# Routed experts in a two-layer kernel: second half routed one step earlier, first group's weight rows spread by DMA out of SBUF instead of DRAM

## Chip, cores and metric

One NeuronCore of a Trainium2 chip. The metric is the device time of one execution in microseconds (us), the median of several. Engines: PE (TensorE), DVE (VectorE), ACT (ScalarE), POOL (GpSimd), and SP (SyncE), which here only issues DMAs. The core has 16 DMA engines.

## The reference

Input `x` has 1024 tokens of 256 numbers. Eight stages follow one another, each of them `x = x + stage(layernorm(x))`:

```
attention A, routed experts, attention B, routed experts,
attention C, small FFN, latent attention, small FFN
```

The change lies in the two "routed experts" stages (same weights both times):

```python
probs = softmax(x @ gate_w)                       # 1024 x 64
top_vals, top_idx = top_k(probs, 8)
rw = zeros(1024, 64); rw[token, top_idx] = top_vals / sum(top_vals)
g = einsum('th,ehi->tei', x, w_gate)              # 64 experts, 256 -> 96
u = einsum('th,ehi->tei', x, w_up)
h = silu(g) * u * rw[:, :, None]
out = einsum('tei,eih->th', h, w_down)            # 96 -> 256, summed over experts
```

All 64 experts are computed for all tokens. `rw` is zero where a token did not choose an expert.

## The kernel before, in words

Class `Moe` holds the expert stage, class `First` the order in which each engine runs it. The two stages are r = 0 and r = 1. The order of work on every engine is written out by hand; engines meet only through semaphores. Each method named below emits instructions on one engine.

**Tiling.** The 64 experts form 16 groups of 4. A group has 4 x 96 = 384 hidden channels, which are 3 blocks of 128 partitions (j = 0, 1, 2), and the tokens are cut in two halves of 512 columns (h = 0, 1). A *unit* is one block and one half, so a group has 6 units, in the order h = 0: j = 0, 1, 2, then h = 1: j = 0, 1, 2. Units 0, 1, 2 of the first group use the first half, units 3, 4, 5 the second.

**One unit.** `gate_up` (PE, L1308) makes 12 matmuls of 128x512, since a float32 product is made of three passes over high and low parts. `activate` (ACT, L1332) takes the silu. `weigh` (POOL, L1357) multiplies it with `e_rw`, the routing weights. `multiply` (DVE, L1377) multiplies with the up part and gives `e_inner`. `high_inner` (ACT, L1338) and `low_inner` (DVE, L1369) split that, and `down` (PE, L1323) makes 6 matmuls. On PE `down` of a unit follows `gate_up` of a unit two later; `gate_up` of unit u waits until `multiply` of unit u-2 is done, because the banks alternate. Beside this, ACT (`high_weights`, L1345) and POOL (`low_weights`, L1364) split one piece of the next group's weights in each unit.

**Routing weights as rows.** `weigh` needs, on each of the 128 partitions of a block, the row of 512 token weights of the expert to which the channel belongs. `e_rw` (128 x 3 x 1024) is that. It is filled by DMA:

- `logits` (PE), `route_begin` (DVE), `route_exp` (ACT), `route_end` (DVE: L1254 to L1264, eight top values, mask, normalization) give the weights of a half of the tokens with tokens on partitions.
- `turn_rows` (PE, L1271) transposes them, `copy_rows` (ACT, L1276) copies them to `rwT`, 64 partitions (one for each expert) x 1024.
- `store_rows` (SP, L1205) writes the half of `rwT` to DRAM, 64 rows of 2 KB, and waits until it has landed.
- `load_rows_of_half` (SP, L1211), for the first group only, reads each of the rows of experts 0 to 3 back, once for each destination partition. The six DMAs (`self.spans`) have 96, 32, 64, 64, 32 and 96 destination partitions: 384 rows of 2 KB, 786,432 bytes for a half.
- `load_rows` (SP, L1217) does the same from DRAM for every later group, with whole rows of 4 KB.

**Order around the change.** First half: its routing is done during the attention stage, `turn_rows` and `copy_rows` right behind it. SP then issues store and loads of half 0 and, in the same queue, the weights of group 1 (`load_group`, L1184 and L1189). Then it waits for half 1. PE runs units 0, 1 and 2 of the first group, between them the logits of the second half. The second half's routing runs on DVE among `multiply` and `low_inner` of units 0 and 1. `weigh` of unit 0 waits for the rows of half 0, `weigh` of unit 3 for those of half 1.

Of the kernel before, what the change touches and what calls it, by code (L numbers as in the profile page):

```python
# [20 lines left out]
HALF = 512  # L21
# [813 lines left out]
class Attend:  # L835
# [178 lines left out]
    def scalar(self, act, hook):  # L1014
# [21 lines left out]
        for what, *args in self.order:  # L1036
            if what == "rows":
                store_rows(*args)
            elif what == "scores":
                exponentiate(*args)  # L1040
            elif what == "store":
                store_sums(*args)
            elif what == "raw":
                self.raws.store(act, *args, self.ring_bank((what, *args)))
            elif what == "values":
                hook(*args)
# [63 lines left out]
class Moe:  # L1110
# [91 lines left out]
    def store_rows(self, sp, r, h):  # L1202
        cols = slice(h * HALF, (h + 1) * HALF)
        sp.wait_ge(self.rows_copied, 2 * r + h + 1)
        sp.dma_start(self.rw_dram[r][:, cols], self.rwT[:, cols]).then_inc(self.rows_stored, 16)  # L1205
        sp.wait_ge(self.rows_stored, 16 * (2 * r + h + 1))

    def load_rows_of_half(self, sp, r, h):
        cols = slice(h * HALF, (h + 1) * HALF)
        for j, e, a, b in self.spans:  # L1210
            sp.dma_start(self.rw[0][a:b, j, cols], self.rw_dram[r][e:e + 1, cols].broadcast_to([b - a, HALF])  # L1211
                         ).then_inc(self.r_first[h], 16)

    def load_rows(self, sp, r, i, s):
# [1022 lines left out]
class First:  # L2237
# [69 lines left out]
    def rows_and_groups(self, sp, r):  # L2307
        moe = self.moe
        first = moe.TURNS * r
        moe.store_rows(sp, r, 0)  # L2310
        moe.load_rows_of_half(sp, r, 0)
        moe.load_group(sp, r, first, 1)
        moe.store_rows(sp, r, 1)
        moe.load_rows_of_half(sp, r, 1)
        moe.load_rows(sp, r, first, 1)
        with sp.Fori(first + 1, first + moe.TURNS) as i:
            for s in range(2):
                moe.load_group(sp, r, i, s)
                sp.wait_ge(moe.weighted, moe.unit(i, moe.UNITS * (s - 1)))
                moe.load_rows(sp, r, i, s)  # L2320
        if r == 1:
            self.c.load(sp)
# [85 lines left out]
    def layer_of_tensor(self, pe, r, proj, ahead):  # L2408

        norm, out, moe, attend, early = self.norm, self.out, self.moe, self.attends[r], self.early[r]  # L2410
        E = self.EARLY
        use = 1 + 2 * r

        def hook(p, j):
            if (p, j) == early["turn"]:
                if r == 0:
                    pe.wait_ge(attend.max_done, attend.maxima)
                pe.wait_ge(attend.ctx_stored, 6)
                out.turn(pe, r, 0, E, attend.ctxs)
            if (p, j) == early["first"]:  # L2420
                if r == 0:
                    pe.wait_ge(proj.wo_loaded, 16)
                out.project(pe, r, 0, E, proj.wo)
            if (p, j) == early["second"]:
                out.project(pe, r, 2, E, proj.wo)
            if (p, j) == early["xT"]:
                norm.turn(pe, use, 0, E)
            if (p, j) == early["logits"]:
                norm.wait_stored(pe, use, 0)
                moe.logits(pe, r, 0, 1)  # L2430

        attend.tensor(pe, proj.wait_stacked, hook, ahead)
        first = moe.TURNS * r
        pe.wait_ge(attend.ctx_stored, 8)
        out.turn(pe, r, 1, (4, 5), attend.ctxs)
        pe.wait_ge(self.start.const_made, Start.CONSTS)
        moe.turn_rows(pe, r, 0, 3)
        out.project(pe, r, 4, (6, 7), proj.wo)
        out.project(pe, r, 6, (6, 7), proj.wo)
        moe.gate_up(pe, r, first, 0)  # L2440
        norm.turn(pe, use, 1, (6, 7))
        pe.wait_ge(moe.rows_copied, 2 * r + 1)
        moe.gate_up(pe, r, first, 1)
        norm.wait_stored(pe, use, 1)
        moe.logits(pe, r, 1, 6)
        moe.gate_up(pe, r, first, 2)
        moe.down(pe, first, 0, first=True)
        moe.down(pe, first, 1)
        moe.turn_rows(pe, r, 1, 7)
        moe.gate_up(pe, r, first, 3)  # L2450
        moe.down(pe, first, 2)
        moe.gate_up(pe, r, first, 4)
        pe.wait_ge(moe.rows_copied, 2 * r + 2)
        for u in range(5, moe.BODY):
            moe.gate_up(pe, r, first, u)
            moe.down(pe, first, u - moe.LAG, first=u == 5)
        with pe.Fori(first + 1, first + moe.TURNS - 1) as i:
            for u in range(moe.BODY):
                moe.gate_up(pe, r, i, u)
                moe.down(pe, i, u - moe.LAG)  # L2460
        last = first + moe.TURNS - 1
        for u in range(moe.BODY):
            moe.gate_up(pe, r, last, u)
            if u == moe.BODY - 1:
                moe.turn_sums(pe, r, 0)
            moe.down(pe, last, u - moe.LAG, final=u == 10)
        moe.down(pe, last, 10)
        moe.down(pe, last, 11, final=True)
        moe.turn_sums(pe, r, 1)
# [288 lines left out]
    def layer_of_vector(self, dve, r, ahead):  # L2758
        norm, out, moe, early = self.norm, self.out, self.moe, self.early[r]
        E = self.EARLY  # L2760
        use, first = 1 + 2 * r, moe.TURNS * r

        def sum_and_gather(t, banks):
            out.add(dve, r, t, banks)
            dve.wait_ge(out.added, 4 * r + t // 2 + 1)
            norm.gather(dve, use, t)
            norm.gather(dve, use, t + 1)

        def hook(p, j):
            if (p, j) == early["copy"]:  # L2770
                for k in range(KC):
                    out.copy_vector(dve, r, 0, k, E)
            if (p, j) == early["first"]:
                sum_and_gather(0, E)
            if (p, j) == early["second"]:
                sum_and_gather(2, E)
            if (p, j) == early["norm"]:
                norm.spread(dve, use, 0)
                norm.invert_by_newton(dve, use, 0)
                for t in range(4):  # L2780
                    norm.scale(dve, use, t)
            if (p, j) == early["xT"]:
                for k in range(KC):
                    norm.store_vector(dve, use, 0, k, E)
            if (p, j) == early["begin"]:
                moe.route_begin(dve, r, 0, 1)
            if r == 1 and (p, j) == (7, 4):
                moe.route_end(dve, r, 0)

        self.attends[r].vector(dve, hook, ahead)  # L2790
        if r == 0:
            moe.route_end(dve, r, 0)
        sum_and_gather(4, (6, 7))
        sum_and_gather(6, (6, 7))
        norm.spread(dve, use, 1)
        norm.invert(dve, use, 1)
        for t in range(4, 8):
            norm.scale(dve, use, t)
        norm.store_vector(dve, use, 1, 1, (6, 7))
        moe.multiply(dve, first, 0)  # L2800
        moe.low_inner(dve, first, 0)
        moe.route_begin(dve, r, 1, 6)
        moe.multiply(dve, first, 1)
        moe.low_inner(dve, first, 1)
        moe.route_end(dve, r, 1)
        moe.multiply(dve, first, 2)
        for u in range(3, moe.BODY):
            self.unit_of_vector(dve, first, u)
        with dve.Fori(first + 1, first + moe.TURNS - 1) as i:
            for u in range(moe.BODY):  # L2810
                self.unit_of_vector(dve, i, u)
        last = first + moe.TURNS - 1
        for u in range(moe.BODY - 1):
            self.unit_of_vector(dve, last, u)
        u = moe.BODY - 1
        moe.low_inner(dve, last, u - 1)
        moe.add(dve, r, 0)
        moe.multiply(dve, last, u)
        moe.add(dve, r, 2)
        moe.low_inner(dve, last, u)  # L2820
        dve.wait_ge(moe.added, 4 * r + 2)
        for t in range(4):
            norm.gather(dve, 2 + 2 * r, t)
# [420 lines left out]
```

## Time and profile before

| | |
|---|---|
| median of 3 runs | 1986.26 us (1985.53 to 1986.53) |
| the profiled execution | 1985.94 us |
| its span | 1984.2 us |
| PE busy | 1830.7 us, 92% |
| DVE, ACT, POOL busy | 1069.4, 919.3, 698.9 us |

A timeline row gives the start of an instruction (or of a run of equal ones) in us from the start of the span, its time in us, engine, line, operation and operands, and in brackets the idle time of the engine before it with what ended it. A row of stretches gives for each engine its busy time with the number of instructions, then the granted PE clock as a share of full speed, the mean busy share of the 16 DMA engines, and the GB/s that they moved. The two expert stages lie at about 208 to 621 us and 779 to 1192 us of the span, their entries at 204 to 240 and 774 to 810 us.

### The profile page before, as it was taken

To read this page: it belongs to the slowest core of one execution; us is meant where nothing else is said; L and a number is where in the kernel's file an instruction comes from. 1 tells how busy PE (TensorE), PEld (TensorE's weight loads), DVE (VectorE), ACT (ScalarE), POOL (GpSimd) and SP (SyncE) were. 2 spreads that over 40 slices of the span, in tenths; PEclk is the share of its full clock that TensorE was granted. 3 is DMA by queue.
4 is the path that set the end of the run, shared out by engine and by line. 5 is a ranking of instruction groups with operands and counts; after the bars stand their busy time and mean duration, and the time that the engine had idled before them with its cause. 6 is when DMAs were issued, how large, how long until landed. Compare 5 with 4: busy or idle time off the path is not lost. (4 is left out here: it accounts for less than half of the span.)

```text
span 1984.2 us, 30249 instructions
## 1 busy us (share of the span) xinstructions
PE 1830.7 (92%) x10564; PEld 1259.1 (63%) x10571; DVE 1069.4 (54%) x1785; ACT 919.3 (46%) x1947; POOL 698.9 (35%) x629
## 2 busy tenths in 40 slices
PE   6999899999998998999999996899979599999997
PEld 3333688888886555788888873333336377777785
DVE  6875444444445654444444456888754255555533
ACT  3676433333334665333333334487743245555521
POOL 5100366666663202566666643300010323232200
PEclk8999999999999999999999999899998599999997
DMA  4300444444430401544444422930010000000000
GB/s 125 89 1 1 126 111 109 110 107 110 108 91 23 114 2 43 136 109 108 108 109 110 110 58 66 135 77 1 1 22 0 0 1 2 1 1 1 1 1 22
DMA packets 136919, 121.71 MB, mean 61 GB/s; under 512 B 84305, under 2 KB 122665, under 8 KB 136585
## 3 DMA queue, kind: packets, MB, share of 16 engines
q1 hardware_dynamic: 136809, 120.24, 24.5%
q8 instruction: 69, 1.13, 0.2%
q14 instruction: 41, 0.34, 0.1%
HBM read 111.41 MB, written 8.65 MB: 61 GB/s over the span
## 5 line engine op out<-in xcount | busy, mean ns | idle before, releaser
L1369 DVE TENSOR_TENSOR e_inner_lo<-e_inner,e_inner_hi 128x512 fp32r<-128x512 f32 x192 | 247.4, 1289 | 390.7 <-ACT e_inner_hi L1338 390.5
L1357 POOL TENSOR_TENSOR e_wsilu<-e_silu,e_rw 128x512 f32<-128x512 f32 x192 | 261.5, 1362 | 225.8 <-ACT e_silu L1332 164.0
L1308 PE MATMUL psum<-e_x_hi,e_w_hi 128*128 128x512 f32 x768 | 304.1, 396 | 7.7 <-DVE e_inner L1377 7.7
L1308 PE MATMUL psum<-e_x_hi,e_w_lo 128*128 128x512 f32 x768 | 299.8, 390 | 0.0
L1308 PE MATMUL psum<-e_x_lo,e_w_hi 128*128 128x512 f32 x768 | 299.5, 390 | 0.0
L1332 ACT ACTIVATE e_silu<-psum 128x512 f32<-128x512 f32 x192 | 114.7, 597 | 346.5 <-PE psum L1308 346.5
L1364 POOL TENSOR_TENSOR e_w_lo<-e_raw,e_w_hi 128x384 fp32r<-128x384 f32 x180 | 221.1, 1228 | 129.1 <-ACT e_w_hi L1345 115.9
L1308 PEld LDWEIGHTS psum<-e_x_hi,e_w_hi 128*128 128x128 f32 x768 | 144.4, 188 | 49.1 <-DVE e_inner L1377 16.9
L1064 DVE TENSOR_REDUCE c_mx<-psum 128x1 f32<-128x1024 f32 x128 | 150.6, 1219 | 28.1 <-PE psum L933 27.6
L1308 PEld LDWEIGHTS psum<-e_x_hi,e_w_lo 128*128 128x128 f32 x768 | 144.6, 188 | 30.8
L1308 PEld LDWEIGHTS psum<-e_x_lo,e_w_hi 128*128 128x128 f32 x768 | 144.7, 188 | 29.1
L1323 PE MATMUL psum<-e_inner_hi,e_w_hi 128*128 128x512 f32 x384 | 150.5, 392 | 10.7 <-DVE e_inner_lo L1369 10.7
L1027 ACT ACTIVATE c_probs<-psum 128x512 f32<-128x512 f32 x256 | 136.4, 601 | 48.0 <-PE psum L965 45.6
L1377 DVE TENSOR_TENSOR e_inner<-psum,e_wsilu 128x512 f32<-128x512 f32 x192 | 130.6, 680 | 47.5 <-POOL e_wsilu L1357 47.5
L1323 PE MATMUL psum<-e_inner_hi,e_w_lo 128*128 128x512 f32 x384 | 149.5, 389 | 0.0
L1323 PE MATMUL psum<-e_inner_lo,e_w_hi 128*128 128x512 f32 x384 | 149.5, 389 | 0.0
L1345 ACT CAST e_w_hi<-e_raw 128x384 fp32r<-128x384 f32 x180 | 92.3, 513 | 122.4 <-PE psum L1323 122.0
L2150 DVE TENSOR_REDUCE l_negmax<-psum 128x1 f32<-128x256 f32 (+7 forms) x128 | 96.9, 757 | 91.3 <-PE psum L1990 90.7
L1338 ACT CAST e_inner_hi<-e_inner 128x512 fp32r<-128x512 f32 x192 | 117.7, 613 | 31.4 <-DVE e_inner L1377 31.4
L2127 POOL TENSOR_TENSOR l_q_whole<-l_rope,l_swap 64x512 f32<-64x512 f32 x32 | 40.8, 1275 | 220.3 <-DVE l_swap L2143 219.1
L2085 ACT COPY xn<-psum 128x512 f32<-128x512 f32 (+2 forms) x96 | 46.0, 480 | 126.6 <-PE psum L2002 126.6
L2077 ACT ACTIVATE l_probs<-psum,l_negmax 128x256 f32<-128x256 f32 (+7 forms) x128 | 95.3, 745 | 18.5 <-DVE l_negmax L2150 16.9
(366 smaller groups left out, 3262.4 us busy)
## 6 DMA issues: line engine op xcount, KB each, us to landing
e_rw<-e_rw_dram SPq DMA_DIRECT2D x60, 384.0 KB, 5.0
e_rw<-e_rw_dram SPq DMA_DIRECT2D x60, 256.0 KB, 5.3
e_raw<-in_L_ffn_w_gate SPq DMA_DIRECT2D x64, 192.0 KB, 2.6
e_raw<-in_L_ffn_w_up SPq DMA_DIRECT2D x64, 192.0 KB, 2.5
e_raw<-in_L_ffn_w_down SPq DMA_DIRECT2D x32, 384.0 KB, 3.5
e_rw<-e_rw_dram SPq DMA_DIRECT2D x68, 128.0 KB, 4.8
c_parts_dram<-c_part SPq DMA_DIRECT2D x8, 384.0 KB, 2.5
a_qs<-a_parts_dram SPq DMA_DIRECT2D x42, 64.0 KB, 2.3
```

Source lines behind the costliest of these rows:

```text
L1027: nc.scalar.activation(self.probs[:, self.step_of[p, j] % 2, x, 0:nq], self.ring_bank(("scores", p, j, x))[:, 0:nq], ACT.Exp, scale=HD ** ...
L1064: nc.vector.tensor_reduce(self.mx[:, p % 2, t % QUART, x:x + 1], self.max_buffer(n)[:, 0:cfg.max_width(t)], AX_X, ALU.max).then_inc(self.m ...
L1308: last = nc.tensor.matmul(bank[u % 2][:], self.w[a][s][:, KC * which + k, j * P:(j + 1) * P], self.x[b][:, k, h * HALF:(h + 1) * HALF], st ...
L1323: last = nc.tensor.matmul(self.obank[2 * h + m][:], flat[:, j * D + m * P:j * D + (m + 1) * P], self.inner_parts[b][:, u % 3, :], start=fi ...
L1332: self.core.nc.scalar.activation(self.silu[:, u % 2, :], self.gbank[u % 2][:], ACT.Silu).then_inc(self.silu_done, 1)
L1338: self.core.nc.scalar.copy(self.inner_parts[0][:, u % 3, :], self.inner[:, u % 2, :]).then_inc(self.high_made, 1)
L1357: self.core.nc.gpsimd.tensor_tensor(self.wsilu[:, u % 2, :], self.silu[:, u % 2, :], self.rw[s][:, j, h * HALF:(h + 1) * HALF], ALU.mult). ...
L1364: self.core.nc.gpsimd.tensor_tensor(self.w[1][1 - s][:, p, :], self.raw[:, p, :], self.w[0][1 - s][:, p, :], ALU.subtract).then_inc(self.w ...
L1369: self.core.nc.vector.tensor_tensor(self.inner_parts[1][:, u % 3, :], self.inner[:, u % 2, :], self.inner_parts[0][:, u % 3, :], ALU.subtr ...
L1377: self.core.nc.vector.tensor_tensor(self.inner[:, u % 2, :], self.ubank[u % 2][:], self.wsilu[:, u % 2, :], ALU.mult).then_inc(self.inner_ ...
L2077: nc.scalar.activation(probs[:, a, t % 2, 0:w], scores_of(a)[:, 0:w], ACT.Exp, bias=negmax[:, n % 4:n % 4 + 1], accum_out=sums[:, t // HT, ...
L2150: nc.vector.tensor_reduce(negmax[:, n % 4:n % 4 + 1], scores_of(a)[:, 0:(t + 1) * P], AX_X, ALU.max, negate=True).then_inc(negmax_ready, 1)
```

## The change

`load_rows_of_half` takes its source from `rwT` in SBUF and no longer from the copy in DRAM: one partition of 512 columns, repeated b - a times by a step of zero. So the loads need no longer wait for the store, and the wait is moved from `store_rows` to a place ahead of `load_rows`, which still reads DRAM. On PE, `turn_rows` of the second half is moved ahead of `down` of unit 1, and on DVE `route_end` of the second half is moved ahead of `low_inner` of unit 1. Number and size of the transfers stay the same.

```diff
         sp.dma_start(self.rw_dram[r][:, cols], self.rwT[:, cols]).then_inc(self.rows_stored, 16)
-        sp.wait_ge(self.rows_stored, 16 * (2 * r + h + 1))
 
     def load_rows_of_half(self, sp, r, h):
         cols = slice(h * HALF, (h + 1) * HALF)
         for j, e, a, b in self.spans:
-            sp.dma_start(self.rw[0][a:b, j, cols], self.rw_dram[r][e:e + 1, cols].broadcast_to([b - a, HALF])
+            sp.dma_start(self.rw[0][a:b, j, cols], self.rwT[e:e + 1, cols].unsqueeze(1).broadcast_to([1, b - a, HALF])
                          ).then_inc(self.r_first[h], 16)
@@ rows_and_groups
         moe.store_rows(sp, r, 1)
         moe.load_rows_of_half(sp, r, 1)
+        sp.wait_ge(moe.rows_stored, 32 * (r + 1))
         moe.load_rows(sp, r, first, 1)
@@ layer_of_tensor
         moe.gate_up(pe, r, first, 2)
         moe.down(pe, first, 0, first=True)
+        moe.turn_rows(pe, r, 1, 7)
         moe.down(pe, first, 1)
-        moe.turn_rows(pe, r, 1, 7)
         moe.gate_up(pe, r, first, 3)
@@ layer_of_vector
         moe.multiply(dve, first, 1)
+        moe.route_end(dve, r, 1)
         moe.low_inner(dve, first, 1)
-        moe.route_end(dve, r, 1)
         moe.multiply(dve, first, 2)
```

## Rows read from the trace of the kernel before

**Rows 1.** Stretches: PE in the steady part of the expert stage, and behind a gap.
```profile
260.00:285.00 25.00, 24.82 (x110) 20.19 (x109) 11.50 (x13) 9.22 (x18) 15.58 (x13) 1.00 0.43 111
803.00:807.00 4.00, 4.00 (x12) 3.10 (x12) 0.00 (x0) 0.00 (x0) 0.64 (x1) 0.57 0.88 247
```

**Rows 2.** Timeline of PE at both entries: start, time, line, operands [idle before <-releaser].
```profile
217.10 0.48 PE L1308 MATMUL psum<-e_x_hi,e_w_hi 128*128 128x512 f32 x1
223.31 0.50 PE L1323 MATMUL psum<-e_inner_hi,e_w_hi 128*128 128x512 f32 x1 [1.83 <-DVE e_inner_lo L1369]
225.67 0.63 PE L1271 MATMUL psum<-ident,xi 128*64 128x128 f32 x4 [0.71 <-DVE xi L1264]
226.05 0.47 PE L1308 MATMUL psum<-e_x_hi,e_w_hi 128*128 128x512 f32 x1
237.46 0.47 PE L1308 MATMUL psum<-e_x_hi,e_w_hi 128*128 128x512 f32 x1 [2.12 <-DVE e_inner L1377]
...
794.37 0.50 PE L1323 MATMUL psum<-e_inner_hi,e_w_hi 128*128 128x512 f32 x1 [2.42 <-DVE e_inner_lo L1369]
808.52 0.47 PE L1308 MATMUL psum<-e_x_hi,e_w_hi 128*128 128x512 f32 x1 [0.50 <-DVE e_inner L1377]
```

**Rows 3.** Timeline of POOL at both entries.
```profile
213.06 1.29 POOL L1357 TENSOR_TENSOR e_wsilu<-e_silu,e_rw 128x512 f32<-128x512 f32 x1 [14.88 <-DMA e_rw<-e_rw_dram]
235.32 1.26 POOL L1357 TENSOR_TENSOR e_wsilu<-e_silu,e_rw 128x512 f32<-128x512 f32 x1 [11.21 <-DMA e_rw<-e_rw_dram]
...
784.73 1.29 POOL L1357 TENSOR_TENSOR e_wsilu<-e_silu,e_rw 128x512 f32<-128x512 f32 x1 [18.83 <-DMA e_rw<-e_rw_dram]
790.01 2.52 POOL L1293 TENSOR_TENSOR e_x_lo<-xT,e_x_hi 128x512 fp32r<-128x512 f32 x2
792.50 1.25 POOL L1357 TENSOR_TENSOR e_wsilu<-e_silu,e_rw 128x512 f32<-128x512 f32 x1
806.36 1.29 POOL L1357 TENSOR_TENSOR e_wsilu<-e_silu,e_rw 128x512 f32<-128x512 f32 x1 [11.18 <-DMA e_rw<-e_rw_dram]
```

**Rows 4.** Timeline of SP's DMA issues at both entries (time is the issue alone).
```profile
204.37 0.52 SPq L1205 DMA_DIRECT2D e_rw_dram<-e_rwT  x1
206.70 3.12 SPq L1211 DMA_DIRECT2D e_rw<-e_rw_dram  x6
226.94 0.51 SPq L1205 DMA_DIRECT2D e_rw_dram<-e_rwT  x1
229.25 3.04 SPq L1211 DMA_DIRECT2D e_rw<-e_rw_dram  x6
...
774.71 0.51 SPq L1205 DMA_DIRECT2D e_rw_dram<-e_rwT  x1
798.00 0.50 SPq L1205 DMA_DIRECT2D e_rw_dram<-e_rwT  x1
```

**Rows 5.** The 24 DMAs of line 1211, time from issue to landing.
```profile
DMA to landing us min/median/max: 2.4/2.8/3.6
```

**Rows 6.** Stretches in which DMAs with different numbers of SBUF partitions run.
```profile
205.00:206.00 1.00, 1.00 (x4) 0.82 (x3) 0.00 (x0) 0.00 (x0) 0.00 (x0) 0.50 0.45 98
231.00:232.00 1.00, 1.00 (x5) 0.82 (x6) 0.00 (x0) 0.00 (x0) 0.00 (x0) 1.00 0.73 238
1217.60:1218.00 0.40, 0.32 (x2) 0.00 (x0) 0.40 (x2) 0.12 (x1) 0.32 (x2) 1.00 1.03 353
1219.00:1219.50 0.50, 0.00 (x0) 0.00 (x0) 0.50 (x2) 0.00 (x0) 0.50 (x1) 1.00 0.16 25
1270.00:1275.00 5.00, 4.91 (x31) 1.34 (x29) 4.61 (x5) 4.12 (x9) 0.00 (x0) 1.00 1.19 123
```

**Rows 7.** Timeline of DVE at the second entry.
```profile
789.88 0.68 DVE L1377 TENSOR_TENSOR e_inner<-psum,e_wsilu 128x512 f32<-128x512 f32 x1
792.87 1.44 DVE L1369 TENSOR_TENSOR e_inner_lo<-e_inner,e_inner_hi 128x512 fp32r<-128x512 f32 x1 [2.30 <-ACT e_inner_hi L1338]
794.23 0.59 DVE L1254 MAX8 xi<-xi 128x8 f32<-128x64 f32 x4
796.25 0.42 DVE L1264 TENSOR_TENSOR xi<-xi 128x256 f32<-128x256 f32 x1
```

## The prediction, made before the kernel ran

> **What bounds the kernel now.** I read the stretches first, then the timeline of each engine at the two entries, then the stretches again for what the DMAs do there.
>
> In the steady part of the expert stage PE is busy 24.82 of 25 us at full clock [rows 1]: it is the bound, and no other engine matters. So the change can only be worth what PE idles at the two entries. In the first, PE waits 1.83, 0.71 and 2.12 us [rows 2], and another 1.9 us behind `gate_up` of unit 3 that the change leaves alone. The 2.12 us is the wait of unit 5 for `multiply` of unit 3, which waits for `weigh` of unit 3 on POOL, which waits for the DMA of the second half's rows [rows 3]. In the second entry the gaps are 2.42 and 0.50 us, and behind them PE runs 4 us at a mean clock of 0.57 [rows 1, 2]. The row DMAs thus sit right behind the bound: `weigh` 0 and 3 start when they land (213.06, 235.32, 784.73, 806.36) [rows 3]. Whatever makes these four transfers longer goes nearly in full to the end of the kernel.
>
> **The transfer out of SBUF.** This decides. Each half moves 384 rows of 2 KB, 0.786 MB. Before, they come from DRAM, at 238 GB/s with engines 0.73 busy [rows 6], about as fast as SP issues them (six in 3.04 us [rows 4]). Now every source row lies in one SBUF partition (0 to 3), and the 16 DMA engines that share a transfer all read that partition. No row shows this, so I go by the nearest ones, and divide GB/s by the busy share to get the rate of 16 fully busy engines [rows 6]:
> - 128 partitions to DRAM (1217.6): 353/1.03 = 343 GB/s.
> - `rwT` to DRAM, 64 partitions (205 to 206): 98/0.45 = 218 GB/s.
> - parts of attention C into 16 partitions at a time (1270 to 1275): 123/1.19 = 103 GB/s.
> - ones from 3 SBUF partitions into 3 others (1219): 25 GB/s in all. Its share, 0.16, is 2.6 of 16 engines, so each engine moves 25/2.6 = 10 GB/s, where one alone moves 343/16 = 21.
>
> The first two have the same direction, SBUF to DRAM: what differs is the number of partitions, and it is the reading side that slows. The fewer partitions, the slower, and the engines stay busy meanwhile: they queue at the memory. If 64 partitions stand behind 8 doors, one door gives 218/8 = 27.2 GB/s, and the last row has 25 GB/s at one. I take 27.2 for a single source partition: 0.786 MB / 27.2 = 28.9 us for a half. Bounds: 31.5 us at 25 GB/s, and at the fast end 0.786 MB / 326 = 2.4 us, if reading one row many times costs no more than it does from DRAM (238/0.73 = 326). Between ends so far apart I take the slow one, since its rows read SBUF and the fast one's does not.
>
> The Trainium skill ("SBUF — State Buffer", section on the DMA port swizzle) has 4 partitions, 0 to 3, behind one port, with 27.6 GB/s measured. By it the half would take 28.5 us, an estimate. The 218 GB/s of the 64-partition store agrees with its eight ports for 64 partitions [rows 6].
>
> Around the bytes come about 2.2 us from issue to landing (the smallest of these DMAs, 64 KB, lands 2.4 us after its issue, 0.2 us of it bytes [rows 5]) and 0.5 us for the issue of the store ahead of it [rows 4]. So rows land 0.5 + 2.2 + 28.9 = 31.6 us after the store's issue. Removing the wait for the store gives back the 2.3 us that the loads were held (229.25 - 226.94 [rows 4]) less that 0.5; it is contained in this sum.
>
> **First half.** Entry 1: 204.37 + 31.6 = 236.0 for `weigh` 0, before 213.06: 22.9 late. Entry 2: 774.71 + 31.6 = 806.3, before 784.73: 21.6 late [rows 3, 4]. What covers it: PE can run `gate_up` 0 and 1 and the logits, then `gate_up` 2 waits for `multiply` of unit 0, so PE stops at 217.10 [rows 2]. Nothing else is there to do. DVE too stands at `multiply` 0, and the whole second routing is queued behind it.
>
> **From `weigh` 0 to the second store.** In entry 2, where `weigh` 0 waited for DMA, this is 798.00 - 784.73 = 13.27 us [rows 3, 4]. The moved routing shortens it. `route_end` starts behind `multiply` 1 (789.88 + 0.68 = 790.56), not at 794.23 [rows 7]: 3.67 us earlier. It is met there by POOL, which is busy from 790.01 to 793.75 [rows 3]. DVE's operations with two SBUF inputs and POOL's exclude one another in this trace: `low_inner` 1 starts at 792.87, ends at 794.31, 0.56 us after POOL's `weigh` ended [rows 3, 7]. The last two operations of `route_end` are of that kind, so 0 to 1.3 us is lost; I take 0.7. PE's `turn_rows`, ahead of `down` 1, falls into the gap that PE has there (2.42 us [rows 2]); `down` 1 waits for `low_inner` 1, which now comes behind `route_end`, at about the time at which POOL lets it in anyway. So 13.27 - 3.0 = 10.3 us.
>
> The group 1 weights are queued behind the rows on the same DMA engines; `high_weights` 0 on ACT waits for the first of them, as in entry 2 now, so this is in the 10.3.
>
> **Second half.** 0.5 + 2.2 + 28.9 again. `weigh` 3 starts at 236.0 + 10.3 + 31.6 = 277.9, before 235.32: 42.6 late. Entry 2: 806.3 + 10.3 + 31.6 = 848.2, before 806.36: 41.8 late [rows 3]. PE has `gate_up` 3 and 4 and `down` 1 and 2 in between, some 10 us, and idles the other 20. The two moves and the removed wait only shorten waits under this one. Behind `weigh` 3 all goes on as before: group 1's rows wait for a store that landed long ago, and land behind the half's rows as before, well ahead of unit 6.
>
> **Clock.** Behind a gap PE has run about 4 us at a mean of 0.57, 1.7 us lost [rows 1]. After idling 20 us I expect at least that in each entry, up to twice that; 2.5 each, less the 1.7 that entry 2 pays already: +3.3.
>
> **Sum.** 42.6 + 41.8 + 3.3 = 87.7 us on the profiled 1985.94, which is 0.3 under the median: 2074 us, slower by 4.4%.
>
> **Rivals.**
> - *The one partition is no bottleneck* (faster). For it: rows read over and over from DRAM lose nothing, and no row has 16 engines on one partition. Against it: the fall from 343 to 218 to 25 GB/s. It decides where a half's bytes take under about 6 us. Then loads start 1.8 us earlier (both halves), the second store another 2.3 to 3.6. Entry 1: `turn_rows` inside PE's gap and no 0.71 wait, so `gate_up` 3 starts 1.25 earlier than 226.05; rows at about 231, so the 2.12 us goes: 3.4. Entry 2: 1.25, the 0.56 by which `down` 1 was later than in entry 1, 0.50, and 1.7 of clock: 4.0 [rows 1, 2]. Time 1979. The Trainium skill ("DMA: Bandwidth & Descriptors", section on bandwidth) binds SBUF-to-SBUF copies only by a fabric limit of 435 GB/s, which speaks for this one; no row here reaches that.
> - *A partition gives twice the rate*, 14.5 us for a half. `weigh` 0 is then 8.5 and 7.2 late, `weigh` 3 13.8 and 13.0 late: 1986 + 27 + 2 = 2015.
> - *One DMA engine carries each transfer*, since the source now has one partition. It moves 343/16 = 21.4 GB/s [rows 6], 36.7 us for a half, 7.8 more in four places: 2105. Against it: the repeat dimension of the source (32 to 96) can be split as before.
> - *The reorder costs*, by DVE and POOL meeting in `route_end`: up to 0.6 us an entry over my 0.7. It alone cannot move the sign.
>
> **Chances.** Forecast 0.73 (own range 2060 to 2092), one engine 0.07, twice the rate 0.05, no bottleneck 0.13, nothing measurable 0.02. The range goes from 2045 (a port rate a quarter above mine, 4 x 7) to 2106 (one engine, or 25 GB/s and double clock loss, 2088). Slower by over 0.2% (4 us; less cannot be told from none): 0.85; within: 0.02; faster: 0.13.
>
> **What would show it.** Row DMAs of line 1211 that take some 30 us to land; DMA share near or over 1 with about 27 GB/s after 206 and again after 246; `weigh` 0 and 3 released by them near 236, 278; two PE gaps of about 20 us in each entry, the first ahead of `gate_up` 2; the second store 10.3 us behind `weigh` 0. It is wrong if these DMAs land in 3 us.

## The result, and the profile after

| | before | changed |
|---|---|---|
| median | 1985.89 us (4 runs, 1984.55 to 1986.53) | 2074.52 us (4 runs, 2072.55 to 2075.18) |
| ratio | | 1.0445 (95%: 1.0433 to 1.0458) |
| profiled execution, span | 1985.94, 1984.2 | 2075.18, 2073.2 |

The kernel is 4.4% slower, as forecast (2074 us). Of all runs in this document one was slow, one of e4's ten (2601.98 us at a granted clock of 0.646), and the ratios leave it out.

The page says little: PE has the same instructions, it only stands still for longer. It is busy for 1844.8 us against 1830.7, part of that work being done at a lower clock behind the gaps, and its share of the span falls from 92% to 89%.

```profile
PE 1844.8 (89%) x10571; PEld 1266.3 (61%) x10571; DVE 1069.5 (52%) x1785; ACT 919.8 (44%) x1947; POOL 698.6 (34%) x629
```

The cause stands in the stretches of the first entry (columns as in [rows 1]).

```profile
206.00:211.00 5.00, 5.00 (x20) 4.14 (x19) 2.19 (x5) 0.00 (x0) 0.00 (x0) 0.79 0.77 48
222.00:234.00 12.00, 0.00 (x0) 0.00 (x0) 0.00 (x0) 0.00 (x0) 0.00 (x0) 0.50 0.90 27
281.00:285.00 4.00, 3.95 (x9) 3.14 (x10) 2.06 (x2) 0.97 (x2) 2.83 (x3) 0.50 1.06 229
```

From 222 to 234 us no compute engine does anything. The 16 DMA engines are 0.90 busy and move 27 GB/s in all. A high busy share beside so low a rate means that packets are under way for long, not that there are many of them. In [rows 6] the same rows came from DRAM at 238 GB/s with a share of 0.73. The last stretch is behind a gap: the granted clock is 0.50, the lower of PE's two levels (1.2 GHz).

SP's issues (against [rows 4]), and the landing time of the 24 row DMAs (against [rows 5]):

```profile
205.88 0.52 SPq L1205 DMA_DIRECT2D e_rw_dram<-e_rwT  x1
206.45 17.64 SPq L1210 DMA_DIRECT2D e_rw<-e_rwT  x6
224.13 9.68 SPq L1184 DMA_DIRECT2D e_raw<-in_L_ffn_w_gate  x2
...
247.61 0.53 SPq L1205 DMA_DIRECT2D e_rw_dram<-e_rwT  x1
248.19 17.63 SPq L1210 DMA_DIRECT2D e_rw<-e_rwT  x6
...
820.88 0.51 SPq L1205 DMA_DIRECT2D e_rw_dram<-e_rwT  x1
862.34 0.52 SPq L1205 DMA_DIRECT2D e_rw_dram<-e_rwT  x1
```

```profile
DMA to landing us min/median/max: 9.5/15.5/17.8
```

The loads are issued 0.57 us behind the store, not 2.3: the wait is gone, as intended. But issuing the six now takes 17.64 us, where it took 3.12, and the two weight loads behind them 9.68. SP is held back for as long as the transfer is slow: in the experiments below, six such issues take 3.8 us where the source is fast (e3, e6), 5.9 in e4 and 14.9 in e5. Queues that are full would explain it; no view shows how full they are.

POOL (against [rows 3]) and PE (against [rows 2]):

```profile
237.11 1.26 POOL L1356 TENSOR_TENSOR e_wsilu<-e_silu,e_rw 128x512 f32<-128x512 f32 x1 [37.20 <-DMA e_rw<-e_rwT]
278.92 1.26 POOL L1356 TENSOR_TENSOR e_wsilu<-e_silu,e_rw 128x512 f32<-128x512 f32 x1 [31.77 <-DMA e_rw<-e_rwT]
...
852.08 1.26 POOL L1356 TENSOR_TENSOR e_wsilu<-e_silu,e_rw 128x512 f32<-128x512 f32 x1 [39.88 <-DMA e_rw<-e_rwT]
893.59 1.26 POOL L1356 TENSOR_TENSOR e_wsilu<-e_silu,e_rw 128x512 f32<-128x512 f32 x1 [30.56 <-DMA e_rw<-e_rwT]
```

```profile
239.15 0.79 PE L1307 MATMUL psum<-e_x_hi,e_w_hi 128*128 128x512 f32 x1 [20.13 <-DVE e_inner L1376]
246.34 0.63 PE L1270 MATMUL psum<-ident,xi 128*64 128x128 f32 x4 [1.39 <-DVE xi L1263]
247.75 0.50 PE L1322 MATMUL psum<-e_inner_hi,e_w_hi 128*128 128x512 f32 x1 [0.78 <-DVE e_inner_lo L1368]
281.05 0.76 PE L1307 MATMUL psum<-e_x_hi,e_w_hi 128*128 128x512 f32 x1 [22.61 <-DVE e_inner L1376]
300.44 0.50 PE L1307 MATMUL psum<-e_x_hi,e_w_hi 128*128 128x512 f32 x1 [0.18 <-DVE e_inner L1376]
...
854.12 0.80 PE L1307 MATMUL psum<-e_x_hi,e_w_hi 128*128 128x512 f32 x1 [20.09 <-DVE e_inner L1376]
895.73 0.76 PE L1307 MATMUL psum<-e_x_hi,e_w_hi 128*128 128x512 f32 x1 [22.80 <-DVE e_inner L1376]
914.96 0.50 PE L1307 MATMUL psum<-e_x_hi,e_w_hi 128*128 128x512 f32 x1 [0.19 <-DVE e_inner L1376]
```

Four gaps of 20.1, 22.6, 20.1 and 22.8 us, 85.6 in sum, each at a `gate_up` that waits for `multiply`, which waits for `weigh`, which waits for the DMA. Cut at the stores that open the entries, the 89.0 us between the spans are: 1.5 ahead of the first (205.88 against 204.37, the same work on both sides), 44.7 from it to the second (615.0 against 570.3), and 42.8 from there to the end (1252.3 against 1209.5). So the two entries hold 87.5 of the 89.0, and the other 1.5 is no effect of the change that anything here shows.

One caution for all comparisons below: the store that opens the first entry lies at 204.37 before, 205.88 here and between 202.61 and 205.93 in the experiments, with the same work ahead of it. So I compare distances from that store, not places.

### The profile page after: what moved, and what is told of

Its sections match the earlier page's. It is cut to its first block and busy times, and to the rows that moved or that the text cites. A ratio compares the mean times of both kernels' runs of the same rounds, so it can differ in the third digit from the quotient of the medians.

```text
span 2073.2 us, 30256 instructions
## 1 busy us (share of the span) xinstructions
PE 1844.8 (89%) x10571; PEld 1266.3 (61%) x10571; DVE 1069.5 (52%) x1785; ACT 919.8 (44%) x1947; POOL 698.6 (34%) x629
## 5 line engine op out<-in xcount | busy, mean ns | idle before, releaser
L1064 DVE TENSOR_REDUCE a_mx<-psum 128x1 f32<-128x384 f32 (+7 forms) x128 | 91.6, 752 | 22.0 <-PE psum L933 21.1
```

What stands on the lines that cost most here:

```text
L1064: nc.vector.tensor_reduce(self.mx[:, p % 2, t % QUART, x:x + 1], self.max_buffer(n)[:, 0:cfg.max_width(t)], AX_X, ALU.max).then_inc(self.m ...
```

## The experiments

Line numbers differ by a few between kernels; the operations are the same.

### Each part by itself

**e1_reorder_only**: the kernel before, with the two moves alone.

```diff
+        moe.turn_rows(pe, r, 1, 7)
         moe.down(pe, first, 1)
-        moe.turn_rows(pe, r, 1, 7)
@@
+        moe.route_end(dve, r, 1)
         moe.low_inner(dve, first, 1)
-        moe.route_end(dve, r, 1)
```

> Only the two moves (turn_rows ahead of down of unit 1 on PE, route_end ahead of low_inner of unit 1 on DVE); the rows still come from DRAM behind the wait for the store. Theory (the whole loss is the transfer from one SBUF partition; the moves bring the second store 3.0 us nearer to weigh 0): store of the second half at about 10.4 us behind weigh 0 in the second entry, weigh 3 3.0 us earlier than before in both entries, DMAs of line 1211 landing in 2.4 to 3.6 us, time 1980 us (1978 to 1982). Rival 1 (the moves cost something by DVE and POOL excluding one another): 1986 or more. Rival 2 (the moves carry part of the 88 us): over 1990.

Measured: 1981.41 us, ratio to before 0.9976 (0.9964 to 0.9989): faster by 0.24%, little but clear of noise, and within the forecast band. Its timeline of SP and POOL in the first entry:

```profile
202.61 0.52 SPq L1205 DMA_DIRECT2D e_rw_dram<-e_rwT  x1
223.03 0.51 SPq L1205 DMA_DIRECT2D e_rw_dram<-e_rwT  x1
```

```profile
212.06 1.30 POOL L1357 TENSOR_TENSOR e_wsilu<-e_silu,e_rw 128x512 f32<-128x512 f32 x1 [15.64 <-DMA e_rw<-e_rw_dram]
231.96 1.29 POOL L1357 TENSOR_TENSOR e_wsilu<-e_silu,e_rw 128x512 f32<-128x512 f32 x1 [9.39 <-DMA e_rw<-e_rw_dram]
```

`weigh` 0 to the second store is 223.03 - 212.06 = 10.97 us, and before 226.94 - 213.06 = 13.88 [rows 3, 4]: 2.9 won. From the first store to `weigh` 3 it is 29.35, before 30.95: 1.6 won, since the two waits from a store to the `weigh` behind it were together 1.3 longer here. In entry 2, `weigh` 0 to the second store is 791.33 - 780.80 = 10.53 us (forecast 10.4), and `weigh` 3 comes 2.6 us earlier (29.07 us behind the first store, before 31.65). So the 3.0 us earlier that I expected of `weigh` 3 came to 1.6 and 2.6. The row DMAs land in 2.4 to 4.4 us, a little over the expected 3.6. The moves are worth some 5 us and carry nothing of the loss.

**e2_source_only**: the changed kernel with the old order of the two moves (the diff of e1 backwards, on the changed kernel).

> Only the new source and the moved wait, the old order on PE and DVE. Theory: row DMAs as in the changed kernel (27 GB/s, some 29 us for a half), weigh 0 at the same place, the second store 13.3 to 13.9 us behind weigh 0 instead of 10.4, so weigh 3 another 3 us later in each entry: 2080.5 us (2079 to 2083). Rival (the moves gain nothing once PE stands still): 2074.5. Rival (the moves cost): below 2074.

Measured: 2080.17 us, ratio 1.0469 (1.0452 to 1.0486), as the theory had it (2080.5).

```profile
234.74 1.27 POOL L1356 TENSOR_TENSOR e_wsilu<-e_silu,e_rw 128x512 f32<-128x512 f32 x1 [37.28 <-DMA e_rw<-e_rwT]
279.01 1.26 POOL L1356 TENSOR_TENSOR e_wsilu<-e_silu,e_rw 128x512 f32<-128x512 f32 x1 [34.14 <-DMA e_rw<-e_rwT]
```

```profile
247.69 0.53 SPq L1205 DMA_DIRECT2D e_rw_dram<-e_rwT  x1
```

`weigh` 0 to the second store is 12.95 us, in the changed kernel 247.61 - 237.11 = 10.50. That is a little under the expected 13.3 to 13.9; in entry 2 it is 864.02 - 850.38 = 13.64. The two parts add up: +94 alone for the source, -5 or -6 for the moves in either setting.

### What about the source is slow

In the next four kernels only the source of the six row DMAs differs from the changed kernel. Bytes, destinations and queue stay the same. They leave out the right routing weights of the first group and put other numbers in their place, so only their times count. A *door* is, as in the prediction, whatever a group of partitions shares on its way to the DMA engines.

**e3_many_partitions**: the source is a constant tile in SBUF, as many partitions as are written.

```diff
-            sp.dma_start(self.rw[0][a:b, j, cols], self.rwT[e:e + 1, cols].unsqueeze(1).broadcast_to([1, b - a, HALF])
+            sp.dma_start(self.rw[0][a:b, j, cols], self.core.wdn[a:b, :, :].rearrange("p k d -> p (k d)")
                          ).then_inc(self.r_first[h], 16)
```

> The changed kernel, but each row DMA reads as many SBUF partitions as it writes (a constant weight tile, partitions a to b, 2 KB each): the routing weights of the first group are left out and replaced by these numbers, all else is computed. Bytes, packets of 2 KB, number of DMAs, destination and issuing queue are those of the changed kernel. Theory (the one source partition is the cause): a half lands within 7 us of the first issue, DMA rate over 200 GB/s, no 20 us gaps, time 1979 us (1977 to 1982). Rival (copies from SBUF to SBUF are slow by themselves, or the destination is): gaps and 2074 us remain.

Measured: 1980.12 us, ratio 0.9970 (0.9957 to 0.9982). All of the loss is gone. So it is not in copying from SBUF to SBUF, not at the destination, and not in SP's order. SP's issue, one stretch, and the landing times:

```profile
224.32 3.79 SPq L1210 DMA_DIRECT2D e_rw<-wdn  x6
```

```profile
225.00:226.00 1.00, 1.00 (x6) 0.84 (x5) 0.00 (x0) 0.00 (x0) 0.00 (x0) 1.00 0.91 215
```

```profile
DMA to landing us min/median/max: 2.0/2.3/2.6
```

**e4_sixteen_partitions**: the source is partitions 0 to 15 of the tile, each repeated.

```diff
-            sp.dma_start(self.rw[0][a:b, j, cols], self.rwT[e:e + 1, cols].unsqueeze(1).broadcast_to([1, b - a, HALF])
+            sp.dma_start(self.rw[0][a:b, j, cols], self.core.wdn[0:16, :, :].rearrange("p k d -> p (k d)").unsqueeze(1).broadcast_to([16, (b - a) // 16, HALF])
                          ).then_inc(self.r_first[h], 16)
```

> The changed kernel, but each row DMA reads the 16 partitions 0 to 15 of a constant weight tile, each repeated 6, 2 or 4 times: the routing weights of the first group are left out and replaced by these numbers. Theory A (groups of partitions share a door of 27 GB/s, as 64 partitions had 218 GB/s and 16 had 103): about 105 GB/s, 7.3 us for a half, weigh 0 about 10 us behind the first store, time 1983 us (1980 to 1986). Theory B (27 GB/s is the limit of one partition by itself): 16 partitions are no limit, over 200 GB/s, as with many partitions, 1979 us.

Measured: 1985.56 us, ratio 0.9993 (0.9983 to 1.0003).

```profile
208.00:210.00 2.00, 2.00 (x11) 1.73 (x10) 1.44 (x3) 0.00 (x0) 0.00 (x0) 1.00 0.94 100
210.00:212.00 2.00, 2.00 (x10) 1.65 (x9) 1.75 (x8) 0.00 (x0) 0.00 (x0) 1.00 0.94 100
```

```profile
DMA to landing us min/median/max: 3.9/4.7/5.5
```

16 neighbouring partitions give 100 GB/s with the engines 0.94 busy, so they queue: 3.7 times the 27 of the changed kernel, not sixteen times. `weigh` 0 comes 10.5 us behind the first store (216.43 - 205.93). Theory A holds. The single partition of the changed kernel gets about what each group of four neighbours would get here (100/4 = 25 GB/s), so it needs no limit of its own.

**e6_sixteen_spread**: 16 partitions again, but every fourth one.

```diff
-            sp.dma_start(self.rw[0][a:b, j, cols], self.rwT[e:e + 1, cols].unsqueeze(1).broadcast_to([1, b - a, HALF])
+            sp.dma_start(self.rw[0][a:b, j, cols], self.core.wdn[0:64:4, :, :].rearrange("p k d -> p (k d)").unsqueeze(1).broadcast_to([16, (b - a) // 16, HALF])
                          ).then_inc(self.r_first[h], 16)
```

> As the run with 16 adjacent partitions, but the 16 source partitions are every fourth one, 0, 4, ... 60 (routing weights of the first group left out, a constant tile read in their place). Same number of partitions, packets and bytes. Theory (neighbouring partitions share a door, four adjacent ones at least): over 200 GB/s at full share and landing in under 3.5 us, against 100 GB/s and 3.9 to 5.5 us with adjacent ones; time 1980 to 1982 us. Rival (the number of source partitions alone sets the rate): 100 GB/s and 1985 us again.

Measured: 1979.96 us, ratio 0.9960 (0.9940 to 0.9981).

```profile
204.26 3.79 SPq L1210 DMA_DIRECT2D e_rw<-wdn  x6
```

```profile
207.00:208.00 1.00, 1.00 (x7) 0.90 (x5) 0.94 (x3) 0.00 (x0) 0.00 (x0) 1.00 0.73 211
```

```profile
DMA to landing us min/median/max: 2.1/2.4/3.5
```

The number of source partitions is that of e4, the place alone differs, and the rate doubles to 211 GB/s at a share of only 0.73: the doors no longer bind, and what the rate meets now is SP's issuing (six in 3.79 us is 0.786 MB / 3.79 = 207 GB/s; e3, with 32 to 96 source partitions, takes the same 3.79 and has about the same rate, 215). Neighbours share one door. This is the sharpest of the four: e4 and e6 differ in one slice. The time (forecast 1980 to 1982) and the landing (forecast under 3.5) come out at the edge of what the theory gave; its "over 200 GB/s at full share" does not hold, since full share is not reached.

**e5_experts_four_apart**: each DMA still reads one partition, but the four experts lie four partitions apart.

```diff
-            sp.dma_start(self.rw[0][a:b, j, cols], self.rwT[e:e + 1, cols].unsqueeze(1).broadcast_to([1, b - a, HALF])
+            sp.dma_start(self.rw[0][a:b, j, cols], self.rwT[4 * e:4 * e + 1, cols].unsqueeze(1).broadcast_to([1, b - a, HALF])
                          ).then_inc(self.r_first[h], 16)
```

> The changed kernel, but the row of expert e is read from partition 4e (0, 4, 8, 12) and not from partition e: the routing weights of the first group are left out and replaced by those of other experts. Each DMA still reads one partition. Theory (at any time the 16 engines all stand at the partition of the DMA that they are working on, since the six DMAs run one after the other): 27 GB/s as in the changed kernel, 2074 us (2068 to 2078). Rival (the four experts' rows being behind one door is what costs; four doors would be used side by side): up to 109 GB/s, 7 us for a half, 1984 us.

Measured: 2043.86 us, ratio 1.0287 (1.0247 to 1.0327). Neither theory: some 31 us less than in the changed kernel, 64 more than with the free sources of e3 and e6.

```profile
206.00:210.00 4.00, 4.00 (x18) 3.04 (x17) 3.33 (x13) 0.67 (x2) 0.00 (x0) 1.00 0.87 26
210.00:214.00 4.00, 3.79 (x21) 2.96 (x21) 1.84 (x5) 3.15 (x5) 0.00 (x0) 1.00 0.88 44
214.00:218.00 4.00, 2.12 (x18) 1.93 (x16) 0.00 (x0) 0.00 (x0) 0.00 (x0) 1.00 0.73 51
```

```profile
211.00:212.00 1.00, 1.00 (x7) 0.79 (x8) 0.47 (x2) 0.75 (x2) 0.00 (x0) 1.00 1.14 94
212.00:213.00 1.00, 1.00 (x6) 0.84 (x5) 0.37 (x1) 0.81 (x3) 0.00 (x0) 1.00 0.75 29
```

```profile
226.72 1.26 POOL L1356 TENSOR_TENSOR e_wsilu<-e_silu,e_rw 128x512 f32<-128x512 f32 x1 [29.69 <-DMA e_rw<-e_rwT]
```

The transfer starts at 26 GB/s; the 44 and 51 behind it are means over bursts. Taken us by us, most of the transfer still runs at 20 to 39 GB/s, with bursts between (94 from 211 to 212, 53 from 214 to 215, 88 from 216 to 217, 66 from 219 to 220). In the changed kernel each us from 208 to 227 has between 16 and 35. Two doors of 27 would give 54, so in the highest bursts more than two are in use. It fits that an engine that has done its share of one DMA goes on to the next, whose row lies behind another door, while others are still at the first. Then the engines would not move in step, as I had supposed; these views don't tell one engine from another, so this is an inference and not shown. The store is at 202.86, so rows are usable 23.9 us behind it, against 237.11 - 205.88 = 31.2 in the changed kernel. So 7.3 us of the changed kernel's 31.2 are there because the rows of all four experts lie side by side.

### One half only

**e7_second_half_only**: the first half comes from DRAM behind the wait, the second from `rwT`.

```diff
+        if h == 0:
+            sp.wait_ge(self.rows_stored, 32 * r + 16)
         for j, e, a, b in self.spans:
-            sp.dma_start(self.rw[0][a:b, j, cols], self.rwT[e:e + 1, cols].unsqueeze(1).broadcast_to([1, b - a, HALF])
+            src = (self.rw_dram[r][e:e + 1, cols].broadcast_to([b - a, HALF]) if h == 0
+                   else self.rwT[e:e + 1, cols].unsqueeze(1).broadcast_to([1, b - a, HALF]))
+            sp.dma_start(self.rw[0][a:b, j, cols], src
                          ).then_inc(self.r_first[h], 16)
```

> The changed kernel, but the first half's rows come from DRAM again, behind the wait for the store; only the second half is read from rwT. Theory (each of the four transfers costs its 29 us less what DRAM took, one after the other, none hides another): weigh 3 some 33 us behind the second store's issue less 1.5, that is 20 us later than before in each entry, 1986 + 40 + 3 = 2030 us (2026 to 2033). Rival (the two halves' stalls overlap, so that one alone costs most of the 88 us): over 2045. Rival (the second half hides behind PE's units 3 and 4): under 2015.

Measured: 2029.96 us, ratio 1.0217 (1.0186 to 1.0247).

```profile
213.72 1.30 POOL L1360 TENSOR_TENSOR e_wsilu<-e_silu,e_rw 128x512 f32<-128x512 f32 x1 [14.50 <-DMA e_rw<-e_rw_dram]
256.75 1.26 POOL L1360 TENSOR_TENSOR e_wsilu<-e_silu,e_rw 128x512 f32<-128x512 f32 x1 [31.75 <-DMA e_rw<-e_rwT]
```

Half of the transfers, half of the loss (44 of 88), and the 2030 that was expected. From the opening store to `weigh` 3 it is 20.4 us longer than before in entry 1 (the store is at 205.41, and 256.75 - 205.41 = 51.3, against 30.95) and 19.1 in entry 2. The stalls add up and neither hides the other, as the order of the program has it: the second half's routing is queued on DVE behind `multiply` 0.

## Why the prediction held, point by point

**The transfer.** Predicted 27.2 GB/s and 28.9 us for a half, rows usable 31.6 us behind the store's issue. Measured 27 GB/s, and 237.11 - 205.88 = 31.2 for the first half, 278.92 - 247.61 = 31.3 for the second; in entry 2 it is 31.2 and 31.3 too, with the store issues at 820.88 and 862.34. What carried this is that one door gives 25 to 27 GB/s. e4 and e6 show the premise that the rate hangs on the doors of the source, which before was only inferred from [rows 6].

That the figure fits to 1% is in part luck. I divided GB/s by the busy share and took eight doors for 64 partitions, a number that no run here counts. The same division gives 27/0.90 = 30 for the changed kernel, and for e6, which isn't held by doors, 211/0.73 = 289, more than the 218 of 64 partitions. So the quotient tells which source is slower, and isn't a fixed property of a door.

One sign of the prediction did not come: its row DMAs were to take some 30 us to land, and they took 9.5 to 17.8 each. Landing counts from the issue of each DMA, and the prediction did not reckon with SP being held back, for 17.6 us over the six. The rows were usable when forecast all the same, since the rate bounds the half as a whole.

**The rivals.** The free source is refuted by the rate of 27 GB/s. e3 shows that its price was right: a source that is free gives 1980, and the rival said 1979. Twice the rate: refuted by 27 GB/s. One engine carrying all: it would show a share of 0.06; the share is 0.90. The cost of the reorder: e1 has a gain instead. In the range, the low end was reckoned wrongly: a rate a quarter above 27.2 saves 5.8 us for a half and not 7, so that case gives 2051 and not 2045. The measured time is far from both.

**From `weigh` 0 to the second store.** Predicted 10.3, measured 10.50 and 862.34 - 852.08 = 10.26. Inside it one term was too small in entry 1, where I took 0.7 us for DVE and POOL excluding one another, bounds 0 to 1.3. DVE there:

```profile
203.44 0.40 DVE L1260 SCALAR_TENSOR_TENSOR xi<-xi 128x256 f32<-128x256 f32 x1
203.87 0.43 DVE L1263 TENSOR_TENSOR xi<-xi 128x256 f32<-128x256 f32 x1
...
244.13 0.74 DVE L1260 SCALAR_TENSOR_TENSOR xi<-xi 128x256 f32<-128x256 f32 x1
244.91 1.37 DVE L1263 TENSOR_TENSOR xi<-xi 128x256 f32<-128x256 f32 x1
246.21 1.48 DVE L1368 TENSOR_TENSOR e_inner_lo<-e_inner,e_inner_hi 128x512 fp32r<-128x512 f32 x1
```

POOL beside it:

```profile
242.06 2.54 POOL L1292 TENSOR_TENSOR e_x_lo<-xT,e_x_hi 128x512 fp32r<-128x512 f32 x2
244.56 1.45 POOL L1356 TENSOR_TENSOR e_wsilu<-e_silu,e_rw 128x512 f32<-128x512 f32 x1
```

The first two rows of DVE are the same operations for the first half, with POOL idle: 0.40 and 0.43 us. Beside POOL they take 0.74 and 1.37, 1.3 lost. The first ends 0.3 us behind POOL's `e_x_lo` (244.60); POOL then starts `weigh`, and the second, started at 244.91, ends 0.3 us behind that (246.01) and so pays again. In entry 2 they take 0.73 and 0.42, 0.3 lost, because POOL was waiting for the silu just then. The mean of both is 0.8.

**Late by how much.** `weigh` 3 predicted 42.6 and 41.8 late. Measured from the opening store: 73.04 us against 30.95 before, 42.1; in entry 2, 893.59 - 820.88 = 72.71 against 806.36 - 774.71 = 31.65, 41.1 late.

**Clock.** This step was wrong in its bookkeeping. Behind `gate_up` of unit 5, PE does the same work up to its next short gap. In the kernel before that gap is here (timeline of PE):

```profile
254.21 0.50 PE L1308 MATMUL psum<-e_x_hi,e_w_hi 128*128 128x512 f32 x1 [0.19 <-DVE e_inner L1377]
...
825.30 0.50 PE L1308 MATMUL psum<-e_x_hi,e_w_hi 128*128 128x512 f32 x1 [0.18 <-DVE e_inner L1377]
```

That is 16.75 and 16.78 us behind `gate_up` 5 [rows 2]. In the changed kernel it is 300.44 - 281.05 = 19.39 and 914.96 - 895.73 = 19.23, so the clock of 0.50 costs 2.6 and 2.5 us. That was my 2.5 each. But I took off 1.7 us that the kernel before pays in entry 2. Those 1.7 lie ahead of `gate_up` 5 there, in time that was spent waiting for `weigh` 3 anyway, so there was nothing to take off: 5.1, not 3.3. The 0.5 and 0.7 by which the lateness was overrated made up for most of it, and 83.2 + 5.1 = 88.3 is the sum by measured terms, against 87.5 in the two entries of the profiled executions and 88.6 between the medians. The mechanism was right but for what was taken off here; that 87.7 came so close to 88.6 is also owed to these two errors being of opposite sign.

## What to carry to other kernels

Ask of a DMA out of SBUF how many separate groups of partitions its source touches. A row repeated out of one partition was the slowest source tried: 27 GB/s, nine times slower than the same row repeated out of DRAM, whose detour costs only a 2.3 us wait. To see it ahead of time, divide GB/s by the DMA busy share in stretches with different partition counts: a quotient that falls with the number of partitions is the warning, though its value is rough (30 and not 27 in the changed kernel). When one change has two parts, time them apart: here the moves alone are 0.24% faster than before (e1, 1981.41 us, the fastest kernel with the full computation), and the source alone 4.7% slower. The free sources of e3 and e6 are not clearly faster than that, so a replicated copy of the rows in SBUF has next to nothing to win here; it wasn't tried.

## What the runs showed of the hardware that I had not expected

- SP is held up by slow transfers: the issue of six row DMAs took 17.6 us instead of 3.1, and DMAs behind them that have nothing to do with the slow source wait in its line (9.68 us for two).
- Where consecutive DMAs read behind different doors, several doors are used at once, but only in bursts (e5: most of the time 20 to 39 GB/s, in single us up to 94). That the DMA engines drift apart would explain it.
- Which partitions a DMA reads counts more than how many: 16 side by side 100 GB/s, 16 four apart 211 GB/s. The Trainium skill ("SBUF — State Buffer", section on the DMA port swizzle) puts partitions 0 to 15 behind four ports and 0, 4, ... 60 behind eight; 100 GB/s agrees with four ports at 25 each, and 211 stays under what eight such would give by the 218 of [rows 6]. Since SP's issuing binds in e6, that run shows more than four doors and doesn't count them.
